# A convolution, linear attention and routed experts on one core: the bias of the convolution added before its product, expert steps of one unit with places per engine, and another order of the first turn

## The reference

```python
x = x + _L0_conv_ref(_gn(x), ...)       # info = relu(Wi x + bi); mask = sigmoid(Wm x + bm)
                                        # relu(Wo (mask (x) info) + bo), 16 x 16 products per pixel
t = _to_tokens(x)
t = t + _L1_attn_ref(_ln_t(t), ...)     # linear attention of 8 heads, elu + 1, two layer norms, an MLP
t = t + _L1_ffn_ref(_ln_t(t), ...)      # 8 experts, softmax gate, the best 2 of 8 weigh gelu(t W1 + b1) W2 + b2
x = _from_tokens(t, x)
```

## Time and profile before

| | |
|---|---|
| median of 3 runs | 1196.23 us (1192.06 to 1196.43) |
| the profiled execution, its own time | 1201.06 us |
| its span | 1199.2 us, 15483 instructions |
| granted TensorE clock, mean | 0.979 |
| PE busy, weight loads (PEld) | 1075.0 us (90%), 497.3 us (41%) |
| DVE, ACT, POOL busy | 783.8 (65%), 681.4 (57%), 359.3 us (30%) |
| chain that ended last | PE 68%, DVE 16%, ACT 12%, issue 3% |
| DMA | 96.64 MB, 81 GB/s in the mean |

### The profile page before, as it was taken

The page is one execution under the profiler, slowest core; times in us unless marked ns, Lnnn a source line. Parts: engine busy times, 40 slices in busy tenths (PEclk is TensorE's granted clock), DMA queues, the critical chain, the costliest instruction groups (busy, mean ns, idle before and its releaser), DMA issues.

```text
span 1199.2 us, 15483 instructions
## 1 busy us (share of the span) xinstructions
PE 1075.0 (90%) x5863; PEld 497.3 (41%) x5878; DVE 783.8 (65%) x1673; ACT 681.4 (57%) x930; POOL 359.3 (30%) x277
## 2 busy tenths in 40 slices
PE   5888759989999899998999989998999989999898
PEld 2454526433554245442453424542354424534232
DVE  4764746588556975488655886659754887547434
ACT  2336345755755656665657656565566555676454
POOL 0100031244312433134322344123431342314465
PEclk9987889999999999999999999999999999999999
DMA  4010069006810095102940059100771019400580
GB/s 148 1 36 1 1 145 211 1 18 132 207 36 18 1 210 129 34 18 53 223 98 1 18 119 219 36 15 4 166 173 36 19 29 222 88 1 18 113 198 27
DMA packets 17418, 96.64 MB, mean 81 GB/s; under 512 B 3648, under 2 KB 6720, under 8 KB 13120
## 3 DMA queue, kind: packets, MB, share of 16 engines
q1 hardware_dynamic: 17344, 95.66, 34.5%
HBM read 77.82 MB, written 9.44 MB: 73 GB/s over the span
## 4 chain that ended last, share of the span: by engine, by line
PE 68%; DVE 16%; ACT 12%; issue 3%; SPq 1%; DMA 0%; DVEq 0%; POOL 0%; POOLq 0%; ACTq 0%
PE HP L809 14%; PE HP L794 12%; PE R L642 7%; PE R L729 5%; ACT H L942 5%; PE R L598 5%; PE R L587 4%; PE R L578 3%; DVE SM L1127 3%; PE R L660 3%; PE R L651 2%; PE R L736 2%; PE R L809 2%; DVE TM L1277 2%; ACT XB L887 1%
## 5 line engine op out<-in xcount | busy, mean ns | idle before, releaser
L988 POOL TENSOR_TENSOR XB<-TM,XB 128x512 f32<-128x512 f32 x254 | 321.3, 1287 | 670.4 <-DVE TM L1277 670.3
L942 ACT ACTIVATE H<-HP,W 128x1024 f32<-128x1024 f32 x224 | 237.6, 1113 | 112.3 <-PE HP L794 111.8
L794 PE MATMUL HP<-XF,W1E 64*128 64x512 f32 x1024 | 256.0, 618 | 24.3 <-DVE TM L1277 23.8
L1277 DVE SCALAR_TENSOR_TENSOR TM<-HP,B2S,CWB 128x512 f32<-128x512 f32 x224 | 161.5, 746 | 132.4 <-PE HP L809 129.1
L809 PE MATMUL HP<-H,W 128*64 128x512 f32 x896 | 226.4, 613 | 22.1 <-ACT H L942 22.1
L794 PEld LDWEIGHTS HP<-XF,W1E 64*128 64x128 f32 x1024 | 87.3, 185 | 148.1 <-DVE TM L1277 82.2
L876 ACT ACTIVATE T<-R 128x512 f32<-128x512 f32 x128 | 73.8, 598 | 101.5 <-PE R L642 89.0
L809 PEld LDWEIGHTS HP<-H,W 128*64 128x64 f32 x896 | 49.4, 135 | 170.6 <-ACT H L942 132.5
L1127 DVE TENSOR_REDUCE SM<-T 128x8 f32<-128x512 f32 x128 | 85.1, 684 | 29.5 <-ACT T L876 27.3
L1099 DVE SCALAR_TENSOR_TENSOR BIG<-R,T 128x512 f32<-128x512 f32 x112 | 70.2, 685 | 30.1 <-PE R L578 29.8
L598 PE MATMUL R<-W,T 128*128 128x128 f32 x512 | 73.4, 289 | 5.7 <-DVE T L1146 5.2
(11 more groups left out here) (165 smaller groups left out, 1363.9 us busy)
## 6 DMA issues: line engine op xcount, KB each, us to landing
CWB<-gates_hbm SPq DMA_DIRECT2D x32, 1536.0 KB, 22.0
CWB<-gates_hbm SPq DMA_DIRECT2D x32, 512.0 KB, 10.0
BIG<-XN SPq DMA_DIRECT2D x32, 256.0 KB, 4.5
out<-XB SPq DMA_DIRECT2D x15, 512.0 KB, 2.9
X<-x SPq DMA_DIRECT2D x14, 512.0 KB, 7.8
W<-wpack SPq DMA_DIRECT2D x1, 1064.0 KB, 5.0
XF<-x SPq DMA_DIRECT2D x2, 512.0 KB, 6.2
gates_hbm<-CWR SPq DMA_DIRECT2D x16, 64.0 KB, 1.6
```

Of the source, the lines that this page charges most:

```text
L794: last = mm(HP[u % BATCH][:, half(k)], W1E[img(k), e, :], XF[img(k), 1 - par, s, half(c)], start=True, stop=True)
L942: f(activated(b, u).rearrange("p k t -> p (k t)"), HP[u % BATCH][:, :], ACT.Gelu, bias=col(B1E + e))\
L988: nc.gpsimd.tensor_tensor(acc, TM[:, u % BATCH, :], acc, ALU.add).then_inc(acc_done, 1)
L1277: v.scalar_tensor_tensor(out=TM[:, u % BATCH, :], in0=sums_of(b, u), scalar=B2S[:, e % 2, e // 2:e // 2 + 1], in1=CWB[:, s, e, half(c)], o ...
```

## The change

Three edits.

**The bias.** ow is scaled by 0.5 once, and LEAST = -bias is set once (DVE, in `prepare`). At the place of `group_norm` ACT adds the bias to X in place, over 128x1024 per slot, after DVE has normalised from it (`gn_done`), and signals `xb_set`. At `conv_out` ACT does nothing; DVE computes max(R, -bias) + (X + bias), which is relu(R + bias) + X, in one operation that reads R from PSUM.

```diff
-                def conv_out(slots):
-
-                    for s, c in pieces(slots):
-                        act.wait_ge(oc_ps[s], at(a + 1, c))
-                        f(T1a[:, s, half(c)], Ra[s][:, half(c)], ACT.Relu, bias=col(B_OUT), scale=0.5).then_inc(oc_act[s], 1)
...
+                def with_bias():
+
+                    for s in range(G):
+                        act.wait_ge(gn_done, nth(a + 1, s))
+                        source = convolution_buffers(a)[0]
+                        f(source[:, s, :], source[:, s, :], ACT.Identity, bias=col(B_OUT)).then_inc(xb_set, 1)
...
+                v.tensor_scalar(w("ow"), w("ow"), 0.5, None, ALU.mult).then_inc(dve_prep, 1)
+                v.tensor_scalar(LEAST[:, :], col(B_OUT), -1.0, None, ALU.mult).then_inc(dve_prep, 1)
...
                 def conv_out(slots):
                     for s, c in pieces(slots):
-                        dve.wait_ge(oc_act[s], at(a + 1, c))
-                        v.tensor_tensor(Xa[:, s, half(c)], Xa[:, s, half(c)], T1a[:, s, half(c)], ALU.add)\
+                        dve.wait_ge(oc_ps[s], at(a + 1, c))
+                        if c == 0:
+                            dve.wait_ge(xb_set, nth(a + 1, s))
+                        v.scalar_tensor_tensor(out=Xa[:, s, half(c)], in0=Ra[s][:, half(c)], scalar=LEAST[:, :], in1=Xa[:, s, half(c)],
+                                               op0=ALU.max, op1=ALU.add)\
                             .then_inc(x1_done[s], 1)
```

```diff
-    ("channel_stats", "H"), ("gates", ""), ("gate_tokens", "Y"), ("gate_exp", ""), ("group_stats", "H"),
...
+    ("channel_stats", "H", 1, 0), ("gates", "H", 0, 0), ("gate_tokens", "YY", 1, 0),
...
+def steps_of(entry, column):
+
+    if column == PE_STEPS:
+        return entry[column]
+    return entry[column] * (FIRST if column == ACT_STEPS else SECOND)
...
-                def expert(step, m):
-                    if step == SECOND:
-                        if last_group(b) and m + 1 < BATCHES:
-                            first_layers(m + 1)
-                        second_layers(m)
-                    elif m == 0 or not last_group(b):
-                        first_layers(m)
...
+                def expert(step, u):
+                    if step == FIRST:
+                        if u < BATCH or not last_group(b):
+                            first_layer(u)
+                        return
+                    if last_group(b) and u % BATCH == 0:
+                        for ahead in range(u + BATCH, min(u + 2 * BATCH, US)):
+                            first_layer(ahead)
+                    second_layer(u)
```

```diff
-    "high_1.0", "high_1.1", "next channel_stats", "conv_out.0", "next group_stats", "conv_out.1",
...
+    "next channel_stats", "info_0.1", "low_0.0", "next group_stats", "high_0.0", "low_0.1", "info_1.0",
+    "high_0.1", "info_1.1", "next group_norm", "low_1.0", "low_1.1", "high_1.0", "high_1.1",
+    "next info_mask_0", "conv_out.1", "conv_out.0", "centre_1.1", "centre_1.0", "rstd_1", "norm_1.1",
+    "next info_mask_1", "next info_0.0", "norm_1.0", "next low_0.0", "features_1.1", "features_1.0",
```

More of the change, by code:

```diff
@@ L84 @@
     "channel_stats", "group_stats", "group_norm", "info_mask_0", "prepare", "info_mask_1", "info_0.0",
[12 rows of a table removed]
-    "gate_tokens", "gate_exp", "choose_1", "next centre_1.0", "choose_2", "gate_rows", "next rstd_1",
-    "next norm_1.1", "next norm_1.0", "next features_1.1", "weights_1", "next features_1.0",
[12 rows of a table added]
+    "gates", "gate_tokens", "gate_exp", "choose_1", "next centre_1.0", "choose_2", "next rstd_1",
+    "gate_rows", "weights_1", "next norm_1.1", "next features_1.1", "next norm_1.0", "next features_1.0",
 ]
@@ L383, in turn @@
                 return
-            at_step = {step: BATCHES - TAIL.count(step) for step in (FIRST, SECOND)}
-            for name, steps in SCHEDULE:
+            at_step = {step: US - TAIL[column].count(step) for step in (FIRST, SECOND)}
+            for entry in SCHEDULE:
+                name = entry[0]
                 if stages.get(name):
@@ L389, in turn @@
                     left, at_step = started, {FIRST: 0, SECOND: 0}
-                for step in steps:
+                for step in steps_of(entry, column):
                     if left:
@@ L813, in expert, with first_layer @@
-                def expert(step, m):
-                    if step == SECOND:
-                        if last_group(b) and m + 1 < BATCHES:
-                            first_layers(m + 1)
-                        second_layers(m)
-                    elif m == 0 or not last_group(b):
-                        first_layers(m)
+                def first_layer(u):
+                    s, e, c = unit(u)
+                    if u == 0 and starting(b):
+                        pe.wait_ge(e_in, 16)
+                    if u < BATCH and starting(b):
+                        pe.wait_ge(cwt_done, 1)
+                    if u % CH_UNITS == 0:
+                        pe.wait_ge(xf_done[s], at(b + 1, LAST))
+                    if last_group(b) and u >= BATCH:
+                        pe.wait_ge(gelu_done, b * US + u + 1 - BATCH)
+                    elif u >= BATCH or exists(b - 1):
+                        pe.wait_ge(comb_done, b * US + u + 1 - BATCH)
+                    for k in range(2):
+                        last = mm(HP[u % BATCH][:, half(k)], W1E[img(k), e, :], XF[img(k), 1 - par, s, half(c)],
+                                  start=True, stop=True)
+                    last.then_inc(l1_ps, 1)
@@ new lines, in second_layer @@
+                def second_layer(u):
+                    s, e, c = unit(u)
+                    pe.wait_ge(gelu_done, b * US + u + 1)
+                    if last_group(b):
+                        if u < FREE:
+                            pe.wait_ge(cwt_done, b + 1)
+                        else:
+                            pe.wait_ge(comb_done, b * US + u + 1 - FREE)
+                    for k in range(2):
+                        last = mm(sums_of(b, u)[img(k), :], w("w2e")[:, C * e:C * e + C], activated(b, u)[:, k, :],
+                                  start=True, stop=True)
+                    last.then_inc(y_ps, 1)
@@ L979, in residual, with add_up, expert @@
                             .then_inc(xs_done[s], 1)
[L981 to L982 removed]
+                def add_up(u):
+                    if last_group(b) and u >= US - BATCH:
                         return
[L984 to L990 removed]
+                    s, e, c = unit(u)
+                    pool.wait_ge(comb_done, b * US + u + 1)
+                    acc = XB[:, 1 - par, s, half(c)]
+                    nc.gpsimd.tensor_tensor(acc, TM[:, u % BATCH, :], acc, ALU.add).then_inc(acc_done, 1)
+                def expert(step, u):
                     if step == SECOND:
[L992 removed]
+                        add_up(u)
                 return slotwise("features_1", residual), expert
[L996 removed]
+            turns(parts, DVE_STEPS)
         @block.vector
```

152 lines of the change are left out of this document (56 added, 96 removed), and 55 rows, old and new, of tables (OPENING, SCHEDULE).

## The result

| | before | changed |
|---|---|---|
| median | 1194.14 us (4 runs, 1191.67 to 1196.43) | 1182.68 us (4 runs, 1182.02 to 1182.90) |
| profiled execution, its span | 1201.06, 1199.2 us | 1182.02, 1180.1 us |
| first turn ends | 160.23 us | 147.34 us |
| second turn | 151.78 us | 151.20 us |
| steady turns | 140.92 us | 139.63 us |

The ratio is 0.9905, 95% interval 0.9884 to 0.9926: 11.5 us faster, where 23 were forecast. (A turn is counted from one group's first `features_1` transposes to the next group's; those are the L613 rows at 53.23 and 160.23 in the earlier trace rows.) The two profiles differ by more than the medians, 19.1 us, because the profiled execution of before lay 7 us over its median.

What follows compares the result with a forecast made beforehand. TensorE was taken as the bound, busy 1075.0 of 1199.2 us, leaving 124.2 to win directly. Terms 2.4 - 16.8 - 9 = -23.4 took 1201.1 to 1177.7 us, scaled by 0.4% to 1173; range 1153 to 1193.

Steps and rivals of the forecast that it cites:

- Steps of one unit: Steady turns: single steps in place of pairs cover TensorE's waits, -2.4 us a turn, -16.8 in 7 turns.
- query.1: Steady turn: the wait of 1.41 us for ACT's copies into XN and XB shrinks to 0.8, -0.6 us.
- the kv_turns, message and the gates' transpose: Steady turn: single layers cover these waits, -1.45 us for both key-value turns and message, -0.7 for the gates.
- hidden: Steady turn: slots go one after the other, so relu's copies and gelus queue on ACT; two waits of 0.2, +0.4 us.
- Router and convolution: Steady turn: the 1.62 us wait stays and gate_rows to conv_out ends within 0.3 us of the old; taken as 0.
- First turn: The first turn's new order fills or shortens gaps and keeps the clock up: -9 us, bounds 0 and -16.
- Fused bias: ACT's two adds ahead of info_mask_0 delay relu, tanh and gelus by 1.0 us: 0.4 in 6 turns, +2.4 us.
- The tail: The part from 1120 us on: same steps in the same order, so 0.
- The larger gain: Rival, chance 0.14: finer places remove all steady-turn gaps but the router chain's 3.9 us; about 1142 us.
- The slower case: Rival, chance 0.08: single gelus at five places between ACT's dense operations hold dense copies back, 4.5 us a turn; 1204 us.
- The fall of the clock in steady turns: Rival, chance 0.04: one slow stretch a turn costs 2.8 us, 19.6 in 7 turns; about 1193 us.
- The prediction's own sign of being wrong: Wrong if steady turns stay at 140.9 us or longer, gelus idle before a waiting dense copy, or the first turn gains most.

Runs made afterwards that it cites:

- steps_only: The kernel before with the new SCHEDULE and its steps of one unit alone, bias and first turn's order as before: 1185.65 us, ratio 0.9913.
- conv_pairs: The changed kernel with the order of before (pairs, slot order 1 then 0) on all engines from gate_rows to conv_out: 1176.40 us, ratio 0.9847.
- paired: The changed kernel with seven pairs of TensorE's single steps side by side again, ACT's and DVE's columns as they are: 1186.83 us, ratio 0.9926.
- open_only: The kernel before with the new order of the first turn (OPENING), nothing else: 1188.13 us, ratio 0.995.
- after_again: The changed kernel measured once more, unaltered: 1180.61 us, ratio 0.9882.
- choose_split: The changed kernel with DVE's choose_2 cut in two and the two combines between the halves: 1182.01 us, ratio 0.9892.
- all_three: The changed kernel with the bias as before, choose_2 cut in two and seven pairs of TensorE's steps rejoined: 1191.68 us, ratio 0.9958.

## Why the prediction was right in sign and too large

**Steps of one unit, forecast -16.8, measured -9.4 alone.** This is the step that failed, and twice: in the size of a turn (-2.4 forecast, -1.3 measured) and in the number of turns (7 forecast; in the profile of steps_only five turns give 6.45, the second turn only 0.6 and the last group's part 0.2). Its waits came out better than forecast: query.1's 1.41 us went entirely (forecast 0.8 left), the kv_turns, message and the gates' transpose as forecast, hidden cost 0.68 instead of 0.4. A steady turn's idle time fell by 3.3 us, where the listed terms come to 1.95 with the bias charge; the sum did not have the waits for combines and gelus behind the router that went too. What the sum left out is that a single step is dearer than half a pair. Twelve first layers and eight second layers stand alone in the changed kernel's steady turn. Six pairs at 0.20 and four pairs at about 0.1 (2 x 0.96 to 1.01 against 1.87) are 1.6 of the 2.0 us by which TensorE's busy time grew. Counted from start to start without the waits, all first layers of a turn take 32.5 us instead of 31.2, all second layers 32.3 instead of 31.8, and everything else together the same. The prediction had the durations of pairs in its rows and halved them ("a first layer (0.96 us)"). The term "Router and convolution", "Taken as 0", failed most clearly: the convolution stretch, which the walk had within 0.3 us of the old, lost 0.98 us, and conv_pairs gave back 0.85 us a turn. The Trainium skill (TensorEngine Tiling (Array Packing), Key Properties) states that changing the tiling mode drains TensorE. The rows fit that: first layers run as 64*128, second layers as 128*64, the replications as 32*128 and most dense products as 128*128, so steps that are cut in two add changes of mode. A steady turn has 63 changes before, 68 in paired, 71 in conv_pairs and 74 in the changed kernel, and TensorE's time without waits is 130.8, 131.6, 132.0 and 132.6 us: 0.15 to 0.17 us for each added change, or 0.1 us a single step. That a drain is the cause was not tested apart; the number of separate stretches of work grows with the changes of mode, and a price of each stretch, whatever its mode, would fit as well.

**First turn, forecast -9 with the end near 151, measured -6.5 in the median, end at 147.3.** `conv_out` starts at 39.97 (forecast about 40), rstd_1 ahead of the gate rows gave 0.9 (forecast 0.8), and L658 got back all of its slow 2.9 us where half was taken. The clock of the last part rose only from 0.77 to 0.86: eight L745 still ran slowly. The end came 12.9 us earlier than in the profile of before, but that profile was an unlucky one. In the three others with the old order the first turn ended at 156.0, 157.4 and 157.5, so between profiles the order is worth 8 to 10 us there. These three executions lay 4.0, 1.0 and 1.7 us over their medians, so the 6.5 us of open_only are the better figure for the median.

**Fused bias, forecast +2.4 (0.4 a turn), measured 0.03 to 0.12 in the usual steady turn, 0.1 to 0.2 in the mean of the five, and +2.75 and +3.3 in all beside its counterpart.** The adds take 1.14 us, over the upper bound of 1.11, DVE's operation 0.751 (forecast 0.745). The relu behind them starts 2.07 us after its product instead of 1.13, 0.9 us later, as forecast (1.0). The second layer's wait grew by 0.9 as the row on ACT let expect. But of "bounds 0 and 1.0" the lower was right: the next first layer waits for a combine in a chain that is full anyway. So that the total comes near +2.4 is luck: the turns that were to pay it give under 1 us, and where the rest arises is not shown. Costing ACT's hop at nothing was right too: thirty-two L603 take 7.09 us in conv_pairs and took 7.09 before.

**The tail, forecast 0**: 81.5 us from the last long wait before, 83.6, 80.8 and 80.1 in kernels with the same instructions there. Between the changed kernel and after_again all of the difference arises in the first 20 us behind that wait, where the clock differs.

**The base.** The sum was made against 1201.1 us and scaled by 0.4%. Where the scatter of before lies is not shown, since it has one profile; that its runs go over 4.8 us and those of open_only over 1.6 points at the first turn, which the new order changes. So scaling the whole was only a stopgap. The bounds 1156 and 1189 leave out the +2.4 of the bias; with it they are 1158 and 1192, and the measured time lies inside both. With measured terms, -6.5 - 9.4 + 3.3 = -12.6, against -11.5 measured first and -14.4 in after_again: the edits add within what the changed kernel itself scatters.

**The rivals.** The larger gain is out: the 3.9 us of the router's chain were not the only thing left, since splitting has a price of its own. The slower case needed gelus that hold a dense copy back; nothing of the kind shows in the steady turn, whose longest new wait but gelu's behind the adds is 0.68 us, at `hidden_1.1`. The fall of the clock in steady turns did not come, with waits up to 1.66 us; with waits of 2.0 us, in two kernels of the study, it did. The prediction's own sign of being wrong, that most of the gain lies in the first turn, is not settled: the profiles have 12.9 of 19.1 us there, with an unlucky one of before, and the single edits give 6.5 us for the first turn's order and 9.4 for the steps.

## What to carry to other kernels

Before cutting a step into smaller ones to fill waits, read what a whole and a half step take from start to start: a wait under the price of the cut (here 0.2 us a pair) is left alone, and the cuts are made only where a wait stands in the trace. Where an engine runs through without a gap, as DVE does here past the router, a delay on another engine beside it cost next to nothing in that stretch and a reordering in it won nothing; less work in it was not tried. What an edit costs in all can still differ from what it costs in that stretch, as with the bias, and is told only by runs beside its counterpart. A forecast from one profile needs to know whether that execution is a typical one.

## What the runs showed of the hardware

Eight matmuls of two steps take 1.92 us from start to start and four 1.06. Behind waits of up to 1.69 us the granted clock never fell in a steady turn. Behind those of 2.0 to 2.1 us it fell in two of choose_split's six turns after the first and in one of all_three's six, and behind those of 2.7 to 2.9 us in the tail in eight of twelve profiles, with the same work behind them at 1.99 to 3.79 us from one execution to the next. ACT's add of a bias from SBUF to SBUF, 128x1024, takes 1.14 us, slightly more than a gelu of that size from PSUM (1.11).
